# A gated graph network's state update in two VectorE operations, with z*h on GpSimd

## The reference, cut to what matters

```python
A = (adj != 0).astype(x.dtype)
h = x
for l in range(5):
    m = jnp.einsum('bnd,de->bne', h, weight[l])
    agg = jnp.einsum('bij,bid->bjd', A, m)
    # gru cell: gi = agg @ w_ih.T + b_ih ; gh = h @ w_hh.T + b_hh ; each split in r, z, n
    r = jax.nn.sigmoid(i_r + h_r)
    z = jax.nn.sigmoid(i_z + h_z)
    n = jnp.tanh(i_n + r * h_n)
    h = (1.0 - z) * n + z * h
x = _layernorm(x + h * mask[..., None])
# then per group g of 5: two symmetric-normalised graph convolutions with ReLU,
# summed with softmax weights, added to x, and normalised again
```

## Time and profile before

| | |
|---|---|
| median of 3 runs | 543.05 us |
| lowest, highest | 537.66, 544.74 us |
| span of the profiled execution | 540.6 us |
| own time of the profiled execution | none given beside its span |
| TensorE (PE) busy | 502.2 us, 93% |
| VectorE (DVE) busy | 467.1 us, 86% |
| ScalarE (ACT) busy | 295.7 us, 55% |
| GpSimd (POOL) busy | 129.5 us, 24% |
| chain that ended last | PE 56%, DVE 23%, issue 14%, DMA 3%, POOL 2% |
| mean granted TensorE clock | 0.992 of full |

### The profile page before, as it was taken

One profiled execution on the slowest core, in us unless ns is written; L12 is line 12 of the kernel. 1 busy time (PEld: TensorE's weight loads), 2 busy tenths in 40 slices (PEclk: granted clock), 3 DMA queues, 4 the chain that ended last, 5 costly groups with the idle time before them and its releaser, 6 DMA issues.

```text
span 540.6 us, 9398 instructions
## 1 busy us (share of the span) xinstructions
PE 502.2 (93%) x2400; PEld 246.0 (46%) x2400; DVE 467.1 (86%) x841; ACT 295.7 (55%) x525; POOL 129.5 (24%) x111
## 2 busy tenths in 40 slices
PE   6998888899999999999999999999989998888795
PEld 5443333344444444444444444444434444444595
DVE  2799999998888888888888888888997999999986
ACT  2555555555656556565564655656544455555674
POOL 2444444400000000000000000000582455566621
PEclk9999999999999999999999999999998999999899
DMA  8998889633222232222223222233831344442102
GB/s 267 303 280 227 222 233 227 162 41 59 39 53 44 39 58 39 56 41 42 55 39 58 39 46 51 39 58 90 192 58 21 78 116 114 112 104 78 48 19 76
DMA packets 122946, 53.03 MB, mean 98 GB/s; under 512 B 86624, under 2 KB 114608, under 8 KB 122928
## 3 DMA queue, kind: packets, MB, share of 16 engines
q1 hardware_dynamic: 121728, 52.29, 41.0%
q10 hardware_dynamic: 1200, 0.53, 0.4%
HBM read 27.63 MB, written 4.19 MB: 59 GB/s over the span
## 4 chain that ended last, share of the span: by engine, by line
PE 56%; DVE 23%; issue 14%; DMA 3%; POOL 2%; DVEq 1%; ACT 1%; SPq 0%; POOLq 0%; ACTq 0%
PE pA L595 16%; DVE E L959 6%; PE pR L601 4%; PE pR L600 4%; PE pR L602 4%; PE pZ L601 4%; PE pZ L602 4%; PE pZ L600 4%; DVE T L974 4%; DVE ST L925 2%; PE pHN L600 2%; PE pHN L601 2%; PE pHN L602 2%; PE pIN L601 2%; PE pIN L600 2%
## 5 line engine op out<-in xcount | busy, mean ns | idle before, releaser
L595 PE MATMUL pA<-A,NAT 128*128 (+1 forms) x640 | 151.1, 379 | 0.9 <-DMA NAT<-HT 0.9
L787 ACT ACTIVATE R<-pR,BRZ 128x512 f32<-128x512 f32 x80 | 54.9, 687 | 118.6 <-PE pR L602 118.3
L595 PEld LDWEIGHTS pA<-A,NAT 128*128 128x128 f16 x640 | 62.5, 98 | 76.6 <-DMA NAT<-HT 1.3
L974 DVE SCALAR_TENSOR_TENSOR T<-pHN,BHN,R 128x512 f32<-128x512 f32 x80 | 59.6, 746 | 25.7 <-ACT R L787 25.7
L802 ACT ACTIVATE NN<-T,COLS 128x512 f32<-128x512 f32 x80 | 57.8, 722 | 42.2 <-DVE T L979 42.2
L527 POOL TENSOR_TENSOR Y<-Y,CM 128x128 f32<-128x128 f32 x5 | 2.6, 551 | 272.5 <-DMA Y<-in_adj_dram 272.5
L959 DVE TENSOR_TENSOR E<-E,Z 128x512 f32<-128x512 f32 x80 | 67.8, 848 | 0.0
L796 ACT ACTIVATE Z<-pZ,BRZ 128x512 f32<-128x512 f32 x80 | 54.7, 684 | 14.8 <-DVE E L959 6.9
L952 DVE TENSOR_TENSOR E<-H,NN 128x512 f32<-128x512 f32 x65 | 44.9, 691 | 19.3 <-ACT NN L802 19.2
L762 ACT ACTIVATE HT<-H (+1 forms) x64 | 39.8, 623 | 37.6 <-DVE H L965 37.6
L979 DVE TENSOR_TENSOR T<-pIN,T 128x512 f32<-128x512 f32 x80 | 55.3, 691 | 2.8
(11 more groups left out here) (148 smaller groups left out, 897.5 us busy)
## 6 DMA issues: line engine op xcount, KB each, us to landing
AS<-in_adj_dram SPq DMA_DIRECT2D x16, 1024.0 KB, 6.0
XS<-in_x_dram SPq DMA_DIRECT2D x30, 256.0 KB, 4.1
out_dram<-Y SPq DMA_DIRECT2D x16, 192.0 KB, 2.1
AS<-in_L_gnn_W_dram SPq DMA_DIRECT2D x2, 640.0 KB, 6.1
NAT<-HT SPq DMA_TRANSPOSE x64, 3.0
out_dram<-Y SPq DMA_DIRECT2D x16, 48.0 KB, 2.2
XS<-in_x_dram ACTq DMA_DIRECT2D x2, 256.0 KB, 5.3
A<-in_L_gnn_weight_dram SPq DMA_DIRECT2D x1, 320.0 KB, 6.5
```

What stands on the lines that cost most here:

```text
L595: last = mm(pA2[:, s % 2, :], NAT[:, s % 2, h, i, :], A16[:, one(b), i, :], start=(h == 0 and i == 0), stop=(h == 1 and i == NI - 1))
L787: nc.scalar.activation(R[:, :], pR[:, :], ACT.Sigmoid, bias=BRZ[:, 0:1], scale=UNSCALE)\
L974: v.scalar_tensor_tensor(out=T[:, :], in0=pHN[:, :], scalar=BHN[:, 0:1], in1=R[:, :], op0=ALU.add, op1=ALU.mult).then_inc(t_v, 1)
```

## The change

GpSimd forms ZH = Z*H in every step, right after Z of that step, with waits on sig_z, on h_v and in layer 0 on hm. ScalarE writes the tanh back into the bank pIN instead of the tile NN. VectorE forms (Z-1)*pIN in that bank, and the new state is ZH - pIN. TensorE's pIN of step k therefore waits for h_v, the state of step k-1, instead of u_v; ScalarE's Z of step k waits also for zh_p, the product of step k-1. The subtraction E = H - NN goes, on VectorE and, in layer 4, on GpSimd. The preparation of the block matrices is cut in pieces, which stand before GpSimd's steps 61, 62, 63, 65 and 66, and VectorE's parts move to its steps 64, 65 and 66. In GpSimd's step ZH stands behind the lo half of x and ahead of the rebuilding of H, the residual sum and the power.

```diff
--- before.py
+++ after.py
@@ -162,8 +162,7 @@
         R = sb("R", [P, N], F32)
         Z = sb("Z", [P, N], F32)
         T = sb("T", [P, N], F32)
-        NN = sb("NN", [P, N], F32)
-        E = sb("E", [P, N], F32)
+        ZH = sb("ZH", [P, N], F32)
 
         WC = sb("WC", [P, L, 2, 3, D], F16)
         WH = sb("WH", [P, 2, 3, D], F16)
@@ -287,7 +286,7 @@
         t_v = sem("t_v")
         u_v = sem("u_v")
         n_a = sem("n_a")
-        d_v = sem("d_v")
+        zh_p = sem("zh_p")
         e_v = sem("e_v")
         h_v = sem("h_v")
         h_hi = sem("h_hi")
@@ -474,14 +473,17 @@
                                         ALU.subtract).then_inc(nat_lo, 1)
 
             def iteration(k, s):
-                if LAST <= s - 1 < K - 1:
-
-                    pool.wait_ge(n_a, k)
-                    pool.wait_ge(h_v, k - 1)
-                    nc.gpsimd.tensor_tensor(E[:, :], H[:, one(graph_of(k - 1)), :], NN[:, :],
-                                            ALU.subtract).then_inc(d_v, 1)
                 if s + 3 < B:
                     natural_lo(k + 3, s + 3)
+                if s < K:
+
+                    if s < B:
+                        pool.wait_ge(hm, k + 1)
+                    if s > 0:
+                        pool.wait_ge(h_v, k)
+                    pool.wait_ge(sig_z, k + 1)
+                    nc.gpsimd.tensor_tensor(ZH[:, :], Z[:, :], H[:, one(graph_of(k)), :],
+                                            ALU.mult).then_inc(zh_p, 1)
                 if s + 2 < B:
 
                     b = graph_of(k + 2)
@@ -511,42 +513,47 @@
                 pool.wait_ge(turn[b], 16)
                 nc.gpsimd.tensor_tensor(H[:, b, :], HT[:, b, 0, :], HT[:, b, 1, :], ALU.add).then_inc(hm, 1)
 
-            def prepare_adjacency():
+            links = [0]
+
+            def link(ins):
+                links[0] += 1
+                ins.then_inc(bd_p, 1)
+                pool.wait_ge(bd_p, links[0])
+
+            def prepare_adjacency(k):
                 g_ = nc.gpsimd
-                n = [0]
-
-                def link(ins):
-
-                    n[0] += 1
-                    ins.then_inc(bd_p, 1)
-                    pool.wait_ge(bd_p, n[0])
-
-                pool.wait_ge(ld_c, 16 * Q)
-
-                for g in range(G):
-                    last = g_.tensor_tensor(AM[:, g, :, :], AB[:, :, :],
-                                            CM[:, g:g + 1, :].to_broadcast([P, NC, S]), ALU.mult)
-                link(last)
-                link(g_.tensor_tensor(AMF, AMF, I32[:, None, :].to_broadcast([P, G * NC, S]), ALU.add))
-                g_.memset(BD[:, :, :, :, :].rearrange("p g c q s -> p (g c q s)"), 0.0).then_inc(am_p, 1)
-
-                pool.wait_ge(deg_v, 1)
-                link(g_.tensor_tensor(DG[1], DG[0], NHALF[:, :], ALU.pow))
-                link(g_.tensor_tensor(DG[2], DG[2], DG[1], ALU.mult))
-                g_.tensor_tensor(AMF, AMF, DG[2][:, :, None].to_broadcast([P, G * NC, S]), ALU.mult).then_inc(am_p, 1)
-
-                pool.wait_ge(deg_v, 2)
-                pool.wait_ge(am_p, 2)
-                for q in range(Q):
-                    rows = slice(S * q, S * q + S)
-
-                    link(g_.tensor_tensor(BD[rows, :, :, q, :].rearrange("p g c s -> p (g c) s"),
-                                            AT[rows, :, :, :].rearrange("p g c m -> p (g c) m"),
-                                            DG[2][rows, :, None].to_broadcast([S, G * NC, S]), ALU.mult))
-
-                assert n[0] == BD_STEPS
-
-            walk(pool, iteration, {62: prepare_adjacency})
+                if k == 61:
+                    g_.memset(BD[:, :, :, :, :].rearrange("p g c q s -> p (g c q s)"), 0.0)
+                elif k == 62:
+                    pool.wait_ge(ld_c, 16 * Q)
+                    for g in range(G):
+                        last = g_.tensor_tensor(AM[:, g, :, :], AB[:, :, :],
+                                                CM[:, g:g + 1, :].to_broadcast([P, NC, S]), ALU.mult)
+                    link(last)
+                elif k == 63:
+                    ins = g_.tensor_tensor(AMF, AMF, I32[:, None, :].to_broadcast([P, G * NC, S]), ALU.add)
+                    ins.then_inc(am_p, 1)
+                elif k == 65:
+                    pool.wait_ge(deg_v, 1)
+                    link(g_.tensor_tensor(DG[1], DG[0], NHALF[:, :], ALU.pow))
+                    link(g_.tensor_tensor(DG[2], DG[2], DG[1], ALU.mult))
+                    g_.tensor_tensor(AMF, AMF, DG[2][:, :, None].to_broadcast([P, G * NC, S]), ALU.mult)\
+                        .then_inc(am_p, 1)
+                elif k == 66:
+                    pool.wait_ge(deg_v, 2)
+                    pool.wait_ge(am_p, 2)
+
+                    pool.wait_ge(zh_p, k)
+                    for q in range(Q):
+                        rows = slice(S * q, S * q + S)
+                        link(g_.tensor_tensor(BD[rows, :, :, q, :].rearrange("p g c s -> p (g c) s"),
+                                              AT[rows, :, :, :].rearrange("p g c m -> p (g c) m"),
+                                              DG[2][rows, :, None].to_broadcast([S, G * NC, S]), ALU.mult))
+                    assert links[0] == BD_STEPS - 1
+
+            for k in range(K):
+                prepare_adjacency(k)
+                iteration(k, k)
             for k in range(K, K + 4):
                 iteration(k, k)
             for part, (c0, c1) in enumerate(PARTS):
@@ -634,7 +641,7 @@
                 split_product(pR, wc(0, 0), wc(1, 0), ag[0], ag[1], False, True).then_inc(r_mm, 1)
                 if s > 0:
 
-                    pe.wait_ge(u_v, k)
+                    pe.wait_ge(h_v, k)
                 split_product(pIN, wc(0, 2), wc(1, 2), ag[0], ag[1], True, True).then_inc(in_mm, 1)
                 split_product(pZ, wc(0, 1), wc(1, 1), ag[0], ag[1], False, True).then_inc(z_mm, 1)
 
@@ -677,7 +684,7 @@
                 if j == 0:
 
                     pe.wait_ge(ld_g, 48)
-                    pe.wait_ge(bd_p, BD_STEPS)
+                    pe.wait_ge(bd_p, BD_STEPS - 1)
                 if g == 0:
 
                     pe.wait_ge(f_nb, Q * c1)
@@ -791,15 +798,12 @@
                         state_hi(k - 1, s - 1)
                     act.wait_ge(z_mm, k + 1)
                     if s > 0:
-
+                        act.wait_ge(zh_p, k)
                         act.wait_ge(e_v, k)
                     nc.scalar.activation(Z[:, :], pZ[:, :], ACT.Sigmoid, bias=BRZ[:, 1:2], scale=UNSCALE)\
                         .then_inc(sig_z, 1)
                     act.wait_ge(u_v, k + 1)
-                    if s > 0:
-
-                        act.wait_ge(h_v, k)
-                    nc.scalar.activation(NN[:, :], T[:, :], ACT.Tanh, bias=BI[:, 2:3], scale=UNSCALE)\
+                    nc.scalar.activation(pIN[:, :], T[:, :], ACT.Tanh, bias=BI[:, 2:3], scale=UNSCALE)\
                         .then_inc(n_a, 1)
 
             act.dma_start(FW[:, :], fusion_w.partition_broadcast(P)).then_inc(ld_f, 16)
@@ -940,29 +944,19 @@
             def iteration(k, s):
                 if 0 <= s - 1 < K:
                     j, b = k - 1, graph_of(k - 1)
-                    h_in = H[:, one(b), :]
                     h_out = H[:, one(b), :] if s - 1 < LAST else HF[:, (s - 1) % 2, :]
-
-                    if s - 1 < LAST or s - 1 == K - 1:
-                        dve.wait_ge(n_a, j + 1)
-                    if s < B - 1:
-
-                        dve.wait_ge(hm, B if s == B - 2 else j + 1)
-                    if s - 1 < LAST or s - 1 == K - 1:
-                        v.tensor_tensor(E[:, :], h_in, NN[:, :], ALU.subtract).then_inc(d_v, 1)
+                    dve.wait_ge(n_a, j + 1)
+                    v.scalar_tensor_tensor(out=pIN[:, :], in0=Z[:, :], scalar=1.0, in1=pIN[:, :],
+                                           op0=ALU.subtract, op1=ALU.mult).then_inc(e_v, 1)
                 if s + 1 < K:
                     aggregated_lo(k + 1, s + 1)
                 if 0 <= s - 1 < K:
-
-                    dve.wait_ge(d_v, j + 1)
-                    dve.wait_ge(sig_z, j + 1)
-                    v.tensor_tensor(E[:, :], E[:, :], Z[:, :], ALU.mult).then_inc(e_v, 1)
-                if 0 <= s - 1 < K:
                     dve.wait_ge(e_v, j + 1)
+                    dve.wait_ge(zh_p, j + 1)
                     if s - 1 >= LAST + 2:
 
                         dve.wait_ge(f_mm, j - LAST - 1)
-                    v.tensor_tensor(h_out, E[:, :], NN[:, :], ALU.add).then_inc(h_v, 1)
+                    v.tensor_tensor(h_out, ZH[:, :], pIN[:, :], ALU.subtract).then_inc(h_v, 1)
                 if s < K:
                     residual_stats(k, s)
                 if s < K:
@@ -1102,7 +1096,7 @@
                                            ALU.subtract, ALU.mult)
                 last.then_inc(z_o, 1)
 
-            walk(dve, iteration, {63: sum_degrees, 64: transpose_adjacency, 65: scale_biases})
```

(1 more changed line is left out.)

## The result

The changed kernel takes 606.05 us (median of 4 runs, 604.35 to 608.64) against 542.83 (median of 4); the ratio is 1.117, with a 95% interval of 1.111 to 1.124. The profiled execution took 608.64; its span is 606.9, against 540.6 before.

The account below looks back on a forecast made before the run. TensorE was taken to bound layers 1 to 3, VectorE's list layers 0 and 4. 0 - 7 + 4 + 58 - 1 = +54 on the 540.6 span, 595; against the median 597, range 576 to 625.

Parts of the forecast that it names:

- Layers 1 to 3: Middle layers: nothing gained or lost, 0, pIN being free 0.21 us before TensorE wants it; ends 0 and +19.
- The rival that turned on this order: Layers 1 to 3 lose too if GpSimd takes the ports before the lo half: +10 to +19, about 610; chance 0.15.
- Layer 0: First layer: VectorE's list gets shorter but the new product meets the cast; -7, ends -14 and 0.
- the -4: Layer 0 with z*h, issued before the cast, holding the ports first: 6.5 us per step, term -4.
- Preparation: Block matrices: one state 6 late behind GpSimd's scaling, block products +1; net +4, ends -1 and +9.
- Layer 4: Last layer: serial chain through four engines, 13 steps, +52, and TensorE's slow clock, +6; together +58, ends +43 and +93.
- the loop over H and pIN: Layer 4: serial chain from one H to the next, 11.06 us per step, 10.9 on average, against 6.94.
- The second loop: Layer 4: pHN to pR and transposes end at 10.7, pIN is wanted at 12.0; counted only as 1.3 us slack.
- the clock's loss: Layer 4: TensorE idle 3.7 us per step, 1.7 lost at low clock, 0.4 to 0.5 uncovered; x 13 = +6.
- The rival of a clock that stays low: Layer 4: TensorE's clock stays low throughout, 14.1 us per step, about 630; chance 0.08.
- Start: Stretch up to T of step 1: the prediction had no term for it.
- Tail: After the last step: one state less work on VectorE, -1.

Follow-up runs that it names:

- e1: The changed kernel with GpSimd's residual sum put ahead of z*h in layer 4, the power still behind it: 577.2 us, ratio 1.066.
- e2: The changed kernel with both the residual sum and the power ahead of z*h on GpSimd: 549.9 us, ratio 1.015.
- e5: The changed kernel with 15 unread products of 512 columns filling TensorE's gap behind the aggregation of steps 67 to 78: 597.2 us, ratio 1.099.
- e6: e4 with the same 15 filling products per step as e5: 592.6 us, ratio 1.092.
- e4: The changed kernel with tanh and (z-1)n in an SBUF tile of their own, pIN no longer waiting for the state: 615.0 us, ratio 1.135.
- e7: e2 with the residual sum also waiting until VectorE has written the variances of graph k-4: 538.0 us, ratio 0.993.
- e3: The kernel before with only layer 4's residual sum also waiting for Z of its step: 583.4 us, ratio 1.077.
- e8: e7 with block transposition, block products and biases' scaling each a step later and layer 0's cast ahead of T: 530.1 us, ratio 0.976.

## Why the prediction was right

It gave 597 and +54 on the span; measured are 606 and +66.3. The sign, the place and the cause hold: z*h in GpSimd's queue ahead of a sum that VectorE wants before T. e1 and e2 show it by order alone (606 to 577 to 550), with the same operations.

*Layers 1 to 3: 0 forecast, +0.4 measured.* pIN was to be free 0.21 before TensorE wants it; the trace has 0.23. z*h was to start behind the lo half of the state, which it does by 0.01 only (252.99 and 253.00), since Z reached GpSimd in 0.14 and not 0.25 (the 0.25 was read in a hardware loop, and GpSimd no longer runs one). The rival that turned on this order was near, and did not come; that the order fell the right way by 0.01 is luck.

*Layer 0: -7 forecast, -4.1 measured.* Of z*h and the cast the one that started first kept its time, and the other's grew by most of what was left of the first: the cast from 1.22 to 2.29 behind the z*h of 67.64, z*h from 1.27 to 2.12 behind the cast of 74.48. The forecast had named both step times, 5.95 and 6.5, but as alternatives; they alternate, since being late puts z*h behind the cast in the next step. By the rule that the first to issue holds the ports (the Trainium skill, SBUF — State Buffer, "Who interferes with whom") the forecast had -4. The trace agrees with the rule, but the -4 took z*h to be first in every step. It was so in every second one, steps 1 to 12 gain 5.3, and the two steps behind them lose 1.2, so that the nearness of -4 and -4.1 is luck in part.

*Preparation: +4 forecast, +4.9 measured.* VectorE waits 6.58 where one state was to be 6 late. The block products cost nothing instead of 1 (z*h of step 66, behind them, still waits 0.22 for Z). TensorE, idle for 6.26 ahead of pIN (409.75), then has a granted clock of 0.50 and 0.55 in the next two windows of 3 us, and no term had that.

*Layer 4: +58 forecast, +62.7 measured.* 11.06 per step with addresses and 10.9 on average were worked out for the loop over H and pIN, and e5, where that loop sets the time, measures 10.56. The second loop (T, pHN, twelve matmuls and the transposes, pIN, pZ, Z, z*h, sum, statistics, T) stands in the working only as a slack, "1.3 of the 1.7 is covered, 0.4 to 0.5 is not". 10.9 less this slack is 9.6, and e6, where the second loop is alone and at the full clock, measures 9.65. In the changed kernel it sets the time, and the clock's loss comes on top of it in full: 11.33 - 9.65 = 1.7 in one step and 12.50 - 9.65 = 2.85 in the next. pHN to pIN shows the same, 4.72 and 5.89 against the 3.03 of e6.

So the term that was mis-sized is the clock's loss. It was taken as 1.7 in every step, from the one idle time of the earlier trace rows; measured are 1.7 and 2.85 in turn, 2.2 on average. 9.6 + 1.7 = 11.3 was forecast per step, the same as 10.9 and the uncovered 0.4; 11.86 was measured. What the forecast did not draw from its own figures is that, with 11.3 above 10.9, the link from H to pIN costs nothing here. It shows in the trace too: z*h was to start 3.4 after HF starts and starts 4.0 after it (492.70, 496.70). That the loop over H was taken 0.3 too long had no effect, which is luck.

e4, e5 and e6 show it: without the link from H to pIN nothing changes (11.84), with the clock kept up 1.3 per step goes (10.56), with both 2.2 (9.65). The rival of a clock that stays low (630) was half right: low behind every gap, but back within the step. Why two steps differ in how long the clock stays low the runs don't say.

*Start: 0 forecast, +2.3 measured.* The first T came at 26.2 in the profile of before and at 27.9 here. With the code ahead of it unchanged it came between 26.4 and 28.1 in e1, e2, e5 and e7, so it differs between executions of one code, and how much of this 1.7 is the change's the runs don't say. The other 0.7 is the change's: from the first T to T of step 1 it is 5.65 in the kernel before and in e3, 6.31 here, and 6.27 to 6.29 in e1, e2, e5 and e7. No term had it.

*Tail: -1 forecast, +0.1.*

## What to carry to other kernels

An operation put into another engine's queue brings its wait along for all that stands behind it. Before moving it, list what follows it in that queue and who waits for that, then follow both ways in which its input depends on the waiter: through the data and through each engine's queue, TensorE's first. Where two loops are near in length, add each up with the clock that its own idle time will bring.

## What the runs showed that was not expected

How long GpSimd holds an operation of VectorE does not depend on that operation's size: NB, 4 elements, lasts 1.01 beside z*h (0.15 alone), X 1.27 (0.34 alone), and the cast 2.29 (1.22 alone). (z-1)n, with one input in the bank, takes 0.69 beside the residual sum (e8, 451.40); in a tile of its own it is held to 1.64 (e4, 82.25). The tanh is written into PSUM in 0.69 against 0.72 into SBUF. And 15 products per step that nobody reads, put into TensorE's gap, made the changed kernel 9 us faster (e5), and e4 22 us (615.0 to 592.6).
